# Two heads in each stack column of 49 rows, with the row-maximum matmuls issued in pairs on 64-row tiles

## What is computed

```python
q, k, v = qkv(x @ Wqkv.T + bqkv)                                  # 16 heads, 16 features each
attn = softmax(einsum('bhid,bhjd->bhij', q, k) / sqrt(16))
coh  = sigmoid(tanh(concat(x, cond) @ Wc1.T + bc1) @ Wc2.T + bc2)  # one value per head and token
mod  = attn * coh / (sum(attn * coh) + 1e-8)
mod  = 0.79 * mod + 0.21 * fa                                     # fa: one softmax per batch
x    = x + (mod @ v) @ Wout.T + bout
x    = x + a map of x that has the same 4x4 quaternion weights for every token
```

## Time and profile before

| | |
|---|---|
| median of 3 runs | 375.09 us (375.02 to 378.11) |
| span of the profiled execution | 375.9 us |
| TensorE, matmuls | 321.0 us busy (85%) |
| VectorE | 223.9 us (60%) |
| ScalarE | 176.9 us (47%) |
| GpSimd | 156.8 us (42%) |
| DMA queue of SP | 34.47 MB, 50.4% of 16 engines |

### The profile page before, as it was taken

How to read it: one execution, slowest core, us unless ns; L and a number is a source line. 1 busy time by engine, 2 the same in 40 slices (tenths; PEclk the granted TensorE clock), 3 DMA queues, 4 the chain that set the end, 5 groups by cost and what they waited for, 6 DMA issues and landing times.

```text
span 375.9 us, 5338 instructions
## 1 busy us (share of the span) xinstructions
PE 321.0 (85%) x1537; PEld 189.0 (50%) x1537; DVE 223.9 (60%) x385; ACT 176.9 (47%) x323; POOL 156.8 (42%) x129
## 2 busy tenths in 40 slices
PE   0848849999799889999799689999799779999975
PEld 0634426555456456655456356655456346544423
DVE  3765943786568616687577407686577517775102
ACT  2101103765356625556456415565356525667750
POOL 9979950099991000299400000199500030296000
PEclk9986975999989958999899958999899969999996
DMA  8698498214953992216924991125943990200001
GB/s 245 247 125 99 146 127 123 83 58 99 125 59 112 126 163 51 75 66 127 124 30 145 149 118 36 62 78 112 118 51 122 124 146 1 84 1 2 1 1 57
DMA packets 16518, 35.87 MB, mean 95 GB/s; under 512 B 2724, under 2 KB 8228, under 8 KB 14456
## 3 DMA queue, kind: packets, MB, share of 16 engines
q1 hardware_dynamic: 14968, 34.47, 50.4%
q10 hardware_dynamic: 1536, 1.23, 1.2%
HBM read 25.07 MB, written 10.50 MB: 95 GB/s over the span
## 4 chain that ended last, share of the span: by engine, by line
PE 63%; DMA 24%; DVE 4%; ACT 3%; issue 3%; SPq 1%; ACTq 0%; DVEq 0%
PE smax_ps L996 14%; PE st_ps L1018 14%; PE o_ps L1030 13%; DMA stack<-max_rows 10%; DMA stack<-qk_scratch 10%; PE job_ps L894 9%; PE job_ps L929 3%; PE job_ps L970 3%; ACT probs L594 2%; DMA qk_scratch<-qk_lo 2%; PE job_ps L951 2%; DVE qk_lo L672 2%; PE smax_ps L982 2%; DMA w_raw<-wqkvT 1%; DVE maxima L746 1%
## 5 line engine op out<-in xcount | busy, mean ns | idle before, releaser
L746 DVE TENSOR_REDUCE maxima<-smax_ps 128x1 f32<-128x512 f32 x256 | 168.3, 686 | 113.6 <-PE smax_ps L996 113.0
L594 ACT ACTIVATE probs<-st_ps 128x512 f32<-128x512 f32 x247 | 142.6, 597 | 137.0 <-PE st_ps L1018 135.6
L996 PE MATMUL smax_ps<-stack 127*128 127x512 f32 x256 | 118.0, 464 | 13.8 <-DMA stack<-qk_scratch 11.9
L1018 PE MATMUL st_ps<-stack 128*128 128x512 f32 x247 | 107.7, 439 | 19.8 <-DMA stack<-max_rows 18.2
L996 PEld LDWEIGHTS smax_ps<-stack 127*128 127x128 f32 x256 | 52.0, 204 | 51.5 <-DVE maxima L746 24.4
L1030 PE MATMUL o_ps<-probs,vals 128*32 128x512 f32 x512 | 71.7, 634 | 1.0 <-ACT probs L594 0.9
L1018 PEld LDWEIGHTS st_ps<-stack 128*128 128x128 f32 x247 | 50.5, 205 | 39.6 <-DMA stack<-max_rows 19.8
L419 POOL TENSOR_TENSOR vals<-v_new,vals 128x256 f32<-128x256 f32 x16 | 10.0, 641 | 94.5 <-PE o_ps L1030 94.5
L401 POOL TENSOR_TENSOR x_lo<-x_raw,x_hi 128x1024 fp32r<-128x1024 f32 x3 | 7.2, 2388 | 65.7 <-ACT x_hi L550 65.7
L894 PE MATMUL job_ps<-x_hi,w_hi 128*128 128x512 f32 x48 | 22.0, 459 | 10.0 <-DVE w_lo L797 9.5
L519 POOL TENSOR_TENSOR prod<-amap,x_tok 128x1024 f32<-128x1024 f32 x12 | 28.6, 2383 | 0.9
(11 more groups left out here) (105 smaller groups left out, 305.5 us busy)
## 6 DMA issues: line engine op xcount, KB each, us to landing
stack<-qk_scratch SPq DMA_DIRECT2D x64, 256.0 KB, 9.7
qk_scratch<-qk_hi SPq DMA_DIRECT2D x16, 256.0 KB, 2.0
qk_scratch<-qk_lo SPq DMA_DIRECT2D x16, 256.0 KB, 2.0
x_tok<-x SPq DMA_DIRECT2D x4, 512.0 KB, 12.0
out<-y SPq DMA_DIRECT2D x8, 256.0 KB, 2.2
x_raw<-xT SPq DMA_DIRECT2D x3, 512.0 KB, 12.1
pe_tab<-fa_rows SPq DMA_DIRECT2D x4, 256.0 KB, 3.8
row<-rows SPq DMA_DIRECT2D x1, 936.0 KB, 7.6
```

The lines of the kernel that those rows point to most:

```text
L594: nc.scalar.activation(probs[:, t % RING, :], st_bank(b, t)[:, :], ACT.Exp, scale=SCALE).then_inc(exp_done, 1)
L746: nc.vector.tensor_reduce(maxima[:, g % 2, n:n + 1], smax_ps[smax_bank(u)][:, :], AX_X, ALU.max).then_inc(smax_reduced, 1)
L996: nc.tensor.matmul(smax_ps[smax_bank(u)][:, :], stack[0:MAX_ROW, 0, h, i * P:(i + 1) * P], stack[0:MAX_ROW, 1, h, :], start=True, stop=Tru ...
L1018: nc.tensor.matmul(st_bank(b, t)[:, :], stack[:, 1, h, j * P:(j + 1) * P], stack[:, 0, h, :], start=True, stop=True).then_inc(st_filled, 1)
```

## The change

- **Layout.** A stack column now holds two heads, one in rows 0 to 48 and one in rows 64 to 112, so `stack` is `[128, 2, 8 pairs, 512]`. `TERMS` is 3 (the product of the two low parts is left out); row 48 of each half holds the maxima and the ones. Of a group's four heads the first two are in the upper half and the other two in the lower (`head_of`).
- **Loads.** `read_stack` issues six DMAs of 128 KB for each group where there were four of 256 KB.
- **Maxima.** `scores_for_max` issues two matmuls at a time, one of each half (48 rows), into two of the three PSUM banks, and only at even steps. It waits until the bank of the second one is reduced too.
- **Row of maxima.** Two DMAs of 4 KB from ScalarE's queue for each group where there was one of 8 KB.
- **Scores.** One matmul at each step as before, with 49 rows of the upper half at even steps and of the lower half at odd steps.
- **Fill.** `blank_rows` is gone, with the wait on it ahead of the DMA of ones; there are two such DMAs.

The diff, cut to its core:

```diff
-TERMS = 4
-ZERO_ROW = TERMS * HD
-MAX_ROW = P - 1
+PAIRS = H // 2
+TERMS = 3
+MAX_ROW = TERMS * HD
+HALF = P // 2
+STACK_DMAS = 2 * TERMS
+def head_of(g, q):
+    return g * HG + (0, 2, 1, 3)[q]
...
-                src = scratch[half].rearrange("n (r h) s -> r n h s", r=HD)[:, :, first:first + HG]
-                dst = stack[:, :, g * HG:(g + 1) * HG, :].bitcast(F32)
-                for t, (q_part, k_part) in enumerate(((1, 2), (1, 3), (0, 2), (0, 3))):
-                    sp.dma_start(dst[t * HD:(t + 1) * HD],
-                                 src[:, q_part:k_part + 1:k_part - q_part]).then_inc(stack_loaded[g], 16)
+                src = scratch[half].rearrange("n (r h) s -> r n h s", r=HD)
+                dst = stack[:, :, 2 * g:2 * g + 2, :].bitcast(F32)
+                for t, (q_part, k_part) in enumerate(((1, 2), (1, 3), (0, 2))):
+                    for side in range(2):
+                        row, head = side * HALF + t * HD, first + 2 * side
+                        sp.dma_start(dst[row:row + HD],
+                                     src[:, q_part:k_part + 1:k_part - q_part, head:head + 2]
+                                     ).then_inc(stack_loaded[g], 16)
...
-            for g in range(G):
-                blank_rows(nc.gpsimd, g).then_inc(zeros_filled, 1)
-            pool.wait_ge(zeros_filled, G)
...
+                for side in range(2):
+                    row = side * HALF + MAX_ROW
+                    act.dma_start(stack[row:row + 1, 0, 2 * g:2 * g + 2, :].bitcast(F32)
+                                  .rearrange("o h (i p) -> o (h i) p", p=P),
+                                  max_rows[side * GS // 2:(side + 1) * GS // 2, :].bitcast(F32)
+                                  ).then_inc(max_loaded, 16)
...
             def scores_for_max(b, u):
                 g, n = u // GS, u % GS
-                h, i = g * HG + n // IT, n % IT
+                pair, i = 2 * g + n // 8, n % 8 // 2
...
-                if not isinstance(b, int) or b or u >= SMAX:
-                    wait(pe, smax_reduced, STEPS * b + u + 1 - smax_before(u))
-                nc.tensor.matmul(smax_ps[smax_bank(u)][:, :], stack[0:MAX_ROW, 0, h, i * P:(i + 1) * P],
-                                 stack[0:MAX_ROW, 1, h, :], start=True, stop=True).then_inc(smax_filled, 1)
+                if not isinstance(b, int) or b or u >= SMAX - 1:
+                    wait(pe, smax_reduced, STEPS * b + max(u + n + 1 - smax_before(u + n) for n in range(2)))
+                for n in range(2):
+                    row = n * HALF
+                    nc.tensor.matmul(smax_ps[smax_bank(u + n)][:, :],
+                                     stack[row:row + MAX_ROW, 0, pair, i * P:(i + 1) * P],
+                                     stack[row:row + MAX_ROW, 1, pair, :],
+                                     start=True, stop=True).then_inc(smax_filled, 1)
...
-                g, j, h = t // GS, t % GS // HG, t // GS * HG + t % HG
+                g, j = t // GS, t % GS // HG
+                pair, row = 2 * g + t % HG // 2, t % 2 * HALF
...
-                nc.tensor.matmul(st_bank(b, t)[:, :], stack[:, 1, h, j * P:(j + 1) * P], stack[:, 0, h, :],
+                nc.tensor.matmul(st_bank(b, t)[:, :], stack[row:row + MAX_ROW + 1, 1, pair, j * P:(j + 1) * P],
+                                 stack[row:row + MAX_ROW + 1, 0, pair, :],
                                  start=True, stop=True).then_inc(st_filled, 1)
...
-                    lead(b, t, following)
+                    if t % 2 == 0:
+                        lead(b, t, following)
                     scores(b, t)
```

More of the change, by code:

```diff
@@ L177, in build @@
         qk_lo = sb("qk_lo", [P, 2, S], F32R)
-        stack = sb("stack", [P, 2, H, S], F32R)
+        stack = sb("stack", [P, 2, PAIRS, S], F32R)
         vals = sb("vals", [P, IT, H, VW])
@@ L280, in job_bank @@
             return job_ps[p.bank(job)], job_filled[p.bank(job)]
-        def blank_rows(eng, g):
-            return eng.memset(stack[ZERO_ROW:P, :, g * HG:(g + 1) * HG, :].bitcast(F32), 0.0)
         block = ctx.enter_context(nc.Block())
@@ L563, in max_row @@
                 ps = filled(p, f"max{g}")
-                wait(act, max_loaded, 16 * (G * b + g))
+                wait(act, max_loaded, 32 * (G * b + g))
                 nc.scalar.activation(max_rows[:, :], ps[0:GS, 0:P], ACT.Copy, scale=-1.0).then_inc(max_rows_done, 1)
                 wait(act, max_rows_done, G * b + g + 1)
-                wait(act, stack_loaded[g], 64 * (b + 1))
-                act.dma_start(stack[MAX_ROW:P, 0, g * HG:(g + 1) * HG, :].bitcast(F32)
-                              .rearrange("o h (i p) -> o (h i) p", p=P),
-                              max_rows[:, :].bitcast(F32)).then_inc(max_loaded, 16)
+                wait(act, stack_loaded[g], 16 * STACK_DMAS * (b + 1))
+                for side in range(2):
[4 more added lines that the diff above has]
+                                  ).then_inc(max_loaded, 16)
             def coherence_hidden(p, b, blk):
@@ L638, in _ @@
             act.wait_ge(ld_fill, 16)
-            act.wait_ge(zeros_filled, G)
-            act.dma_start(stack[MAX_ROW:P, 1].bitcast(F32),
-                          fill_copy.unsqueeze(1).to_broadcast([1, H, S])).then_inc(ones_filled, 16)
+            for half in range(2):
+                row = half * HALF + MAX_ROW
+                act.dma_start(stack[row:row + 1, 1].bitcast(F32),
+                              fill_copy.unsqueeze(1).to_broadcast([1, PAIRS, S])).then_inc(ones_filled, 16)
             ps = filled(FIRST, "field_logits")
@@ L745, in reduce_scores @@
                 wait(dve, smax_filled, STEPS * b + u + 1)
-                nc.vector.tensor_reduce(maxima[:, g % 2, n:n + 1], smax_ps[smax_bank(u)][:, :], AX_X,
+                at = n % 2 * (GS // 2) + n // 2
+                nc.vector.tensor_reduce(maxima[:, g % 2, at:at + 1], smax_ps[smax_bank(u)][:, :], AX_X,
                                         ALU.max).then_inc(smax_reduced, 1)
@@ L989, in scores_for_max @@
                 g, n = u // GS, u % GS
-                h, i = g * HG + n // IT, n % IT
+                pair, i = 2 * g + n // 8, n % 8 // 2
                 if n == 0:
-                    wait(pe, stack_loaded[g], 64 * (b + 1))
-                if not isinstance(b, int) or b or u >= SMAX:
-                    wait(pe, smax_reduced, STEPS * b + u + 1 - smax_before(u))
-                nc.tensor.matmul(smax_ps[smax_bank(u)][:, :], stack[0:MAX_ROW, 0, h, i * P:(i + 1) * P],
-                                 stack[0:MAX_ROW, 1, h, :], start=True, stop=True).then_inc(smax_filled, 1)
+                    wait(pe, stack_loaded[g], 16 * STACK_DMAS * (b + 1))
+                if not isinstance(b, int) or b or u >= SMAX - 1:
[6 more added lines that the diff above has]
+                                     start=True, stop=True).then_inc(smax_filled, 1)
             def lead(b, t, following):
@@ L1006, in scores @@
             def scores(b, t):
-                g, j, h = t // GS, t % GS // HG, t // GS * HG + t % HG
+                g, j = t // GS, t % GS // HG
+                pair, row = 2 * g + t % HG // 2, t % 2 * HALF
                 if t % GS == 0:
-                    wait(pe, max_loaded, 16 * (G * b + g + 1))
+                    wait(pe, max_loaded, 32 * (G * b + g + 1))
                 if spread(b, t):
@@ L1028, in weigh_values @@
                     wait(pe, o_raw_done, G * b + g)
-                for h in range(HG):
-                    ins = nc.tensor.matmul(o_ps[h * VW:(h + 1) * VW, :], vals[:, j, g * HG + h, :],
-                                           probs[:, (HG * n + h) % RING, :], start=(j == 0), stop=(j == IT - 1))
+                for q in range(HG):
+                    h = head_of(0, q)
+                    ins = nc.tensor.matmul(o_ps[h * VW:(h + 1) * VW, :], vals[:, j, head_of(g, q), :],
+                                           probs[:, (HG * n + q) % RING, :], start=(j == 0), stop=(j == IT - 1))
                 ins.then_inc(av_done, 1)
@@ L1109, in _ @@
             pe.wait_ge(ld_wc2, 16)
-            pe.wait_ge(ones_filled, 16)
+            pe.wait_ge(ones_filled, 32)
             for u in range(LEAD):
@@ L1121, in _ @@
                     maxima_rows(FIRST, 0, 0)
-                scores_for_max(0, u)
+                if u % 2 == 0:
+                    scores_for_max(0, u)
             front(FIRST, 0, True, False)
```

4 lines of the change are left out of this document (2 added, 2 removed).

## The result

| | before | after |
|---|---|---|
| median of 4 runs each | 376.60 us (375.02 to 380.67) | 412.37 us (407.54 to 427.76) |
| ratio, 95% interval | | 1.0997 [1.0852, 1.1141] |
| span of the profiled execution | 375.9 us | 409.9 us |
| mean granted clock in it | 0.904 | 0.779 |
| TensorE busy | 321.0 us (85%) | 371.5 us (91%) |

The account below looks back on a forecast made before the run. TensorE's own queue was taken to bound the kernel, alternating with two DMA waits a pass. -9.2 - 3.6 - 9.2 - 4.0 - 2.0 + 3.2 + 2.0 = -22.8 us on 375.9 gave 353.1, as median 352.5; range 337 to 378.

Parts of the forecast that it names:

- Stack loads: Loads of 768 KB for 1 MB a group: 8.9 us for 11.2, TensorE waiting 4 x 2.3 = 9.2 us less.
- Row of maxima: The small DMA of maxima lands sooner behind group 2's shorter load, in setup and each pass: 9.2 us less waiting.
- 2.3 us earlier, four times: Row's landing behind group 2's load, scaled by bytes: (10.9 - 1.8) x 0.25 = 2.3 us, four times, 9.2 us.
- a rival for the row getting ahead of the tokens: Maxima issued ahead of tokens land 2.5 us earlier still in passes 2 and 3, clock holds: 342.5 us, chance 0.15.
- The clock behind the waits: Shorter waits keep the clock up: 3.6 us gained behind stack waits in three passes, 4.0 behind pass 1's row wait.
- Pairs: Two 64-row maxima matmuls run side by side in 0.235 us, saving 7.5 us of TensorE time a batch.
- pairs one after the other: Rival: the pairs' 7.5 us a batch don't come, the changes of size do: 364.5 us, chance 0.13.
- Changes of tile size: Between score matmuls, weighings and inserted jobs: 0.10 us each, 68 changes a pass, 6.8 us.
- dearer changes: slower: Rival: each change of tile size empties the array at 0.40 us instead of 0.10: 402 us, chance 0.15.
- Jobless stretches: Steps without other jobs: ScalarE's turn covers the pairs' saving, so four steps still take 3.3 us.
- VectorE: A pair waits for the maximum before the last to be reduced: 0.5 us a batch, 2 us lost (bounds 0 and 8).
- ScalarE's second DMA: 16 more DMAs issued from ScalarE's queue behind weighings, 0.2 us late each: 3.2 us lost (bounds 0 and 9).

Follow-up runs that it names:

- kernel with later tokens: Kernel before with three 16-row blocks (768 KB a group) and full tiles, SP issuing the token load behind group 3's stack load: 347.7 us, ratio 0.922.
- kernel with pieces at even steps: Kernel after with seven of 24 projection thirds moved from odd steps to the even step next to them: 398.0 us, ratio to before 1.048.
- the fastest kernel: Kernel before with 768 KB loads, full tiles, later token loads, and setup's group 3 and tokens issued once the first row of maxima landed: 343.7 us, ratio 0.911.
- three blocks: Kernel before with the product of the low parts left out, 768 KB a group in three DMAs, 128-row tiles kept: 362.0 us, ratio 0.966.

## Why the prediction was wrong, point by point

I forecast 352.5 us with a range to 378, and gave "slower" 0.15. It is 412.4. Two steps failed: the clock, for which the sum had only gains and no term for 64-row tiles, cost 28.7 us or more; and a change of tile size, put at 0.10 us, costs 0.195.

**Stack loads: right.** Foretold were 9.2 us less of waiting; it was 11.9 - 2.4 = 9.5. In the passes group 0 lands 7.9 to 8.2 us after its first issue, where it was 11. TensorE began to wait for it 8.6 us after that issue before the change, so nothing was left to wait for, although in after it comes only at 11.1 us or later. In the setup the first matmul starts 8.0 us after the first issue (17.38 to 25.43), where I had 8.8 to 8.9 and before had 11. With full tiles, 256 KB a DMA and the same bytes it is 9.1 (21.46 to 30.55, in the kernel with later tokens), so scaling by bytes held, and the 96 issues cost nothing; the finer ones are 1 us quicker, a gain I had as a bound.

**Row of maxima: right where the queue ahead of it stayed the same.** By my scaling it had to land 13.4 - 2.3 = 11.1 us after the load's first issue in passes 2 and 3; with the same bytes and full tiles it is 11.1. Of the waits foretold, 2.7, 0.4, 2.9 and 3.0, the last two came in that kernel (2.90, 2.97), but its setup had 8.3 and its pass 1 3.19. The step "2.3 us earlier, four times" took the transfers ahead of the row as given. In that kernel, with fewer issues for a group, the tokens in pass 1 and group 3 in the setup got ahead of it. I had a rival for the row getting ahead of the tokens and none for the reverse. In after the waits fall by 17 us, where I had 9.2, and much of that surplus is no gain. In the setup the row lands 10.9 us after the load's first issue (40.92 to 51.83) as before, and the wait is 0.96 us for 5.00 because TensorE comes 4.0 us later to it. In pass 2 it lands 9.7 us after (220.24 to 229.91), 3.7 sooner than before, and TensorE comes 1.3 us later. In passes 1 and 3 TensorE comes after it has landed.

**The clock behind the waits: wrong in kind.** I put down -3.6 and -4.0 us for a clock that holds once the waits are short, and nothing else. I had taken from the earlier trace rows that the clock falls behind a wait, and read this as "falls when TensorE is idle, so it holds when TensorE is busy". No row of before had 64-row matmuls in number, so none could show the other cause, and I named no rival for it. This is the missing term, and the largest. Its size: in the last batch 26.3 us were lost. In jobless steps all of the 1.65 us in each four is the clock; behind the maxima it is 8.9 of 11.4. In batch 0 to 1, 14.6 us were lost, and with the clock held up by added matmuls 12.3 of them come back (82.1 us), although 32 added matmuls stand in it. In the first eight intervals of the last batch they bring back 7.5 (39.2 for 46.7 us). 12.3 + 7.5 + 8.9 = 28.7 us is the least that the clock cost, if the added matmuls save nothing else; without it the kernel would be at 384 us or lower. The most is half of the time at 0.50, (1 - 0.779) x 409.9 = 91 us, of which before has (1 - 0.904) x 375.9 = 36 too. The share can't be given closer, since no kernel had after's work at 2.4 GHz throughout.

The Trainium skill, TensorE: Matmul & The Clock Gate, Part 1, says that the gate is set by how busy TensorE has been recently, 2.4 GHz when busy. The trace disagrees for small tiles: busy for 100.00 of 100 us, the clock was 0.50. That rule is what I had leaned on without naming it.

**Pairs: right.** I took 0.235 us for a pair, without changes of size. With a change ahead of it it takes 0.34, and second-pass matmuls pair as well (0.32), which I hadn't foreseen. The rival "pairs one after the other" is out.

**Changes of tile size: sized at half.** 0.10 us was read from the two sides of the weighing; measured is 0.195 for each change. The row I relied on the earlier trace rows shows only what sticks out at a weighing. In after a job starts 0.43 us behind a single score matmul (205.53, 205.96), where I had named 0.33 as the sign, the next job 0.33 us behind it and the pair 0.33 us behind that (206.29, 206.62), for 0.235: each change leaves some 0.10 us on two spacings and I had counted one. With 68 changes a pass the missing 0.095 us is 6.5 us, and over the 170 exposed changes of my own count 16 us; both are reckoned, not measured. The kernel with pieces at even steps gives 1.9 to 3.8 us a pass for seven sites. The pass loses at full clock too: take from after's 82.2 us half of its 13.9 us at 0.50 and 75.2 are left, where the fastest kernel, with full tiles and the clock at 1.00, takes 72.4. Of the 2.8 us between them 1.6 can be after's waits for the maxima. The rival "dearer changes: slower" was to decide from 0.23 us a change. The changes stayed below that, so it is not this rival that came true, though its sign did.

**Jobless stretches: right at 2.4 GHz** (3.33 us, foretold "still 3.3"), and beside the point at 1.2 GHz (4.98).

**VectorE: undersized.** Foretold 2 us, the waits of pairs for `maxima` sum to 12.5 us in 23 waits. In the jobless steps the 0.54 us of it lie where ScalarE's turn used to lie and cost nothing (3.33 against 3.34). What the rest costs wasn't isolated, nor was ScalarE's second DMA (foretold 3.2 us).

**What I said would prove me wrong** didn't quite appear: the waits for `maxima` are 12.5 us, not tens, and the load's landing moved as foretold. The list lacked the check that mattered, the clock in a stretch where TensorE doesn't wait.

## What to carry to other kernels

A matmul on 64-row tiles can run beside another, but two things go against it: each change between tile sizes costs 0.195 us at 2.4 GHz, where a whole matmul of 512 columns takes 0.235, and for long stretches a stream of such matmuls ran at 1.2 GHz here while TensorE was never idle. If fewer rows are needed, keep the 128-row tile with zeros below, as here with three blocks, and take the gain from the smaller transfers. When transfers are made fewer or shorter, look again at the order of issue: a small transfer that the next wait hangs on may now stand behind others. And take a wait that shrank for a gain only when its transfer landed sooner; here some of them shrank because TensorE came later.

## What the hardware showed that was not expected

- **Clock.** At 0.50 with TensorE busy for all of 100 us (48- and 49-row matmuls, one at a time), all of 30 us (64-row and 128-row in turn), 96% of 56 us (pairs). The code with 64-row matmuls in turn had 0.98 with 65 rows, and one 128-row matmul added ahead of each pair gave 1.00. That the tile and not the rows that hold data decides follows from 64 against 65 rows, and from the kernels that fill the same rows and read 127 and 128 (mean clock 0.911 and more) or 48 and 49 (0.767 and less); that changes of size between scores aren't needed for it, from the kernel that had none. What remains open is when it falls: in after's passes with projections it comes and goes, the alternation of 64 and 128 rows had 1.00 from 394 to 440 us, the single 48- and 49-row matmuls had it among projections from 360 to 400, and executions of one kernel with 19 added matmuls had mean clocks from 0.786 to 0.871. At the very end of the last batch the 49-row matmuls and weighings ran at 2.4 GHz both in after (from 389 us) and in the kernel with 19.
- **Changes of tile size.** 0.195 us each at 2.4 GHz (0.43 against 0.235 us from matmul to matmul, the same over a run of them). The Trainium skill, TensorEngine Tiling (Array Packing), Key Properties, says that changing the tiling mode drains TensorE; the runs agree in that each change costs time, and give its size.
- **Pairs in fp32r.** Two 64-row matmuls of 512 columns take 0.34 us from the entry of the first to that of the next, with a change of tile size in it, and so 0.24 without the 0.10 that the change leaves there.
